# Two LayerNorms of the last four batches normalised on ScalarE, the routing maximum read from PSUM

## The chip, the cores and the metric

The kernel runs on one core of a Trainium2 chip. TensorE (PE) multiplies matrices, VectorE (DVE), ScalarE (ACT) and GpSimd (POOL) work element by element, and SyncE (SP) issues the DMAs. Each engine takes its instructions in the order in which the program gives them to it; between engines only semaphores order the work. The metric is the time of one execution on the device, in microseconds (us).

## The reference

Eight sequences (batches) of 128 tokens with 512 features pass through a two-layer decoder of six sublayers. Each sublayer is added to its input, and the sum is normalised over its features:

```python
def _layernorm(x, axis=-1, eps=1e-05):
    m = jnp.mean(x, axis=axis, keepdims=True)
    v = jnp.var(x, axis=axis, keepdims=True)
    return (x - m) / jnp.sqrt(v + eps)
...
    x = _layernorm(x + _L0_attn_ref(x, ...), axis=-1)              # stage 0
    x = _layernorm(x + _L0_xattn_ref(x, ctx_4096, ctx_4096), axis=-1)  # stage 1
    x = _layernorm(x + _L0_ffn_ref(x, ...), axis=-1)               # stage 2
    x = _layernorm(x + _L1_attn_ref(x, ...), axis=-1)              # stage 3
    x = _layernorm(x + _L1_xattn_ref(x, ctx_4096, ...), axis=-1)   # stage 4
    x = _layernorm(x + _L1_ffn_ref(x, L1_ffn_route_w, L1_ffn_A, L1_ffn_Bw), axis=-1)  # stage 5
```

Stages 4 and 5 matter here. Stage 4 is an attention with 32 query heads on 8 key and value heads, whose output is projected by `Wo`. Stage 5 sends each token to the one of eight low-rank experts with the largest logit:

```python
        logits = jnp.einsum('bsd,ed->bse', x, route_w)
        topk_v, topk_idx = jax.lax.top_k(logits, 1)
        route_weight = jax.nn.one_hot(topk_idx[..., 0], E, dtype=logits.dtype) * topk_v
        h = jnp.einsum('bsd,erd->bser', x, A)
        wh = route_weight[..., None] * h
        out = jnp.einsum('bser,eor->bso', wh, Bw) * SCALING
```

## The kernel before

The whole decoder is one program of five instruction streams, written out by hand; what stands in a stream is done in that order. `x_tok` holds all eight batches in SBUF, tokens on the 128 partitions and 512 features in the free dimension, and is updated in place by every stage. HB is 4, half of the batches.

Stage 4 runs in slots. Slot s, from 0 to 63, is one batch of one key head in one half of the batches (NU is 16 heads over both halves, so NU*HB is 64). The loop is pipelined over the slots on each engine: in slot s the scores of s are computed, the weights of s-1 are turned, the values of s-2 are multiplied and the projection by `Wo` of s-4 is added up in PSUM. The loop goes on to slot 71 (SLOTS is 72) to drain. In slots 64 to 67 the projections of the last four batches (4 to 7) are completed, and stage 5 of these batches runs in steps that `routed_at(s)` gives out, one batch after the other, a slot apart: step 0 turns x (PE line 883, ScalarE copies it out as `x5T`), step 1 multiplies by the experts' first matrices and the route (PE line 892), and DVE chooses the expert in `route` (lines 1971 to 1978), step 2 turns the weighted result `wh` (PE line 897, ScalarE copies it out as `whT`), step 3 multiplies by the second matrices (PE line 900), and DVE adds and normalises. Step 0 of batch 4 is in slot 65, step 3 of batch 4 in slot 68, that of batch 7 in slot 71. Within a slot the steps of the earlier batch come first. The first four batches go through the same steps one at a time in slots 40 to 55, beside the attention of the others.

A LayerNorm has two parts on DVE. `ln_a` adds the sublayer's result to x (line 1574), takes the statistics (1576, 1577) and adds epsilon to the variance (1578). POOL raises that to the power -0.5 in `rstd` (line 1322). `ln_b` waits for POOL and then subtracts the mean and multiplies (line 1582), in one instruction. In slots 64 to 71 `ln_b` follows its `ln_a` at once, so that DVE waits there for POOL. What else stands in DVE's stream there: `o_rest`, the rest of the attention's output that ScalarE's rounding leaves (line 1964), for s-2, at the head of slots 64 and 65. PE's step 0 of batch 4 waits for the last `o_rest` too:

```python
                    elif rb == HB and step == 0:
                        pe.wait_ge(S.t_sb, NU * HB)
                        pe.wait_ge(S.o_sb, NU * HB)
```

ScalarE's copies out of PSUM all go through one helper, so that the profile has them all at line 968; they are told apart by their tiles. `o_split` is the rounded part of the attention's output, and `x5T` and `whT` are parts of `arena` (128x512 and 128x128). SP stores each batch when its `x_done` has come (line 490), in order.

Of the kernel before, what the change touches and what calls it, by code (L numbers as in the profile page):

```python
# [15 lines left out]
P = 128  # L16
B = 8
# [115 lines left out]
def decoder_kernel(nc, xT, xtok, ctxT, ctxtok, par, rows, four, win, wx, wdt, wout, qw, sc, ze,  # L133
                   loraA, loraBT, dwin, dw1, dw2, dwout, wq, wk, wv, wo, ra, bwT, out):
    scratch = nc.dram_tensor("bc_scratch", [2, NS, HT], F32, kind="Internal").ap()
    with ExitStack() as ctx:
# [33 lines left out]
        lnmv = sb("lnmv", [P, B, 2])  # L170
        lnve = sb("lnve", [P, B])
        lnrs = sb("lnrs", [P, B])
        halfneg = sb("halfneg", [P, 16])

        def pc(name):
# [203 lines left out]
        def by_dve(k, c):  # L379

            return c == 1 and k % 4 == 2

        def weighed(k, c):

# [581 lines left out]
        def _(act):  # L966
# [304 lines left out]
            def routed(b, step, bk):  # L1271
# [6 lines left out]
                else:  # L1278
# [2 lines left out]
                        act.wait_ge(S.rf_ps, b)  # L1281
                    av(whT, bank[bk][:, 0:P], ACT.Identity).then_inc(S.whT_done, 1)

            for j in range(GQ):
                query_out(0, j)
                split_q(j + 3)
                if j % 2:
                    keys_values(KV_LAST + 3 + j // 2)
            for s in range(SLOTS):
# [16 lines left out]
                if 2 <= s < NU * HB + 2:  # L1306
                    r = s - 2
                    rv, rb = r // HB, r % HB
                    act.wait_ge(S.av_ps, r + 1)
                    if r >= 3:  # L1310
                        act.wait_ge(S.op_ps, r - 2)

                    av(osp[:, 0, r % 3, :], bank[3][:, :], ACT.Identity,
                       bias=pc("bv")[:, rv % NKV:rv % NKV + 1]).then_inc(S.o_hi, 1)
                for rb, step, bk in routed_at(s):
                    if step in (0, 2):
                        routed(rb, step, bk)

        def rstd(pool, stage, b):

# [4 lines left out]
        def _(pool):  # L1325
# [164 lines left out]
            for b in range(B):  # L1490
                rstd(pool, 3, b)
                if b >= HB:
                    rest_q(b - HB + 3)

            for s in range(SLOTS):
                if s < 2 * NKV * HB:
                    rest_q(s + 7)
                    rest_of(wos[:, 1, s % 8, :], wo_sb[:, s % 3, :], wos[:, 0, s % 8, :], S.wo_hi, s + 1, S.wo_lo)
                for b in range(B):
                    if s == (0 if b < HB else (NKV - 1) * HB) + b % HB:  # L1500
                        bias(b, 2 * B + b, "bo")
                rv, b = (s - 4) // HB, (s - 4) % HB
                if rv % NKV == NKV - 1 and 4 <= s < 2 * NKV * HB + 4:
                    rstd(pool, 4, (rv // NKV) * HB + b)
                for rb, step, bk in routed_at(s):
                    if step == 3:
                        rstd(pool, 5, rb)

        @block.vector
        def _(dve):  # L1510
# [56 lines left out]
            def ln_a(stage, b, ps, ready, value):  # L1567
# [7 lines left out]
                dve.wait_ge(S.x_sum, lnc(stage, b))  # L1575
                link(v.bn_stats(lnst[:, b, :], x_tok[:, b, :]))
                link(v.bn_aggr(lnmv[:, b, :], lnst[:, b, :]))
                v.tensor_scalar(lnve[:, b:b + 1], lnmv[:, b, 1:2], 1e-5, None, ALU.add).then_inc(S.ln_ve, 1)  # L1578

            def ln_b(stage, b):  # L1580
# [387 lines left out]
            def route(b):  # L1968

                dve.wait_ge(S.r_ps, b + 1)  # L1970
                link(v.tensor_copy(logits, bank[2][:, P:P + 8]))
                link(v.max(rt8, logits))
                link(v.max_index(ri8[:, :], rt8, logits))
                link(v.tensor_copy(rif, ri8[:, :]))
                link(v.tensor_scalar(rwt, pc("iota8"), rif[:, 0:1], rt8[:, 0:1], ALU.is_equal, ALU.mult))
# [8 lines left out]
            for s in range(SLOTS):  # L1984
# [8 lines left out]
                if 4 <= s < NU * HB + 4:  # L1993
                    r = s - 4
                    rv, rb = r // HB, r % HB
                    if rv % NKV == NKV - 1:
                        b = (rv // NKV) * HB + rb
                        ln_a(4, b, bank[4 + rb][:, :], S.op_ps, r + 1)
                        ln_b(4, b)
                for rb, step, bk in routed_at(s):  # L2000
                    if step == 1:
                        route(rb)
                    elif step == 3:
                        ln_a(5, rb, bank[bk][:, :], S.rf_ps, rb + 1)
                        ln_b(5, rb)


# [69 lines left out]
```

## Time and profile before

| | us |
|---|---|
| Median of 3 runs | 1402.76 |
| Lowest, highest | 1397.98, 1403.25 |
| The profiled execution | 1402.18 |
| Its span, from the first instruction to the last event | 1400.4 |
| PE busy in the span | 1289.2 (92%) |
| DVE busy | 927.4 (66%) |
| ACT busy | 731.3 (52%) |
| POOL busy | 646.5 (46%) |

The shares are averages over stages with different limits. A row of the timeline gives the start of an instruction from the start of the span, its duration, the engine, the line, the tiles that it writes and reads with their shapes, and in brackets how long the engine was idle before it and whose work ended that. A row of the table of windows gives busy time and number of instructions of each engine in one stretch; PEclk is the clock granted to TensorE as a share of its full 2.4 GHz. A matmul with 32-bit operands is shown as two records.

### The profile page before, as it was taken

The numbers are of one execution on the slowest core, as the hardware profiler recorded it, in microseconds if no ns is written. First come the engines' busy times: TensorE is split into PE (matmuls) and PEld (weight loads), VectorE is DVE, ScalarE is ACT, GpSimd is POOL, SyncE is SP. The second block draws the span as 40 slices with busy tenths as digits, with TensorE's granted clock in tenths as the row PEclk, the third lists the DMA queues.
The fourth block names the chain that finished last, engine by engine and source line by source line (L and its number), as shares of the span: only waits on it lengthen the run. The fifth ranks groups of instructions, "written<-read, shape, count | busy, mean of one in ns | idle before, by whom it ended". The sixth has DMA issues, their size and how long they took to land.

```text
span 1400.4 us, 18312 instructions
## 1 busy us (share of the span) xinstructions
PE 1289.2 (92%) x6432; PEld 929.4 (66%) x6432; DVE 927.4 (66%) x1690; ACT 731.3 (52%) x1407; POOL 646.5 (46%) x471
## 2 busy tenths in 40 slices
PE   7996887888899899989999999999998999999996
PEld 6874766666667664443655555778787778778774
DVE  4775898999988877795545535654444465555566
ACT  5579999899988841211232232544444335444441
POOL 4128988898888812213711113623332433333221
PEclk9998999999999999998999999999999999999999
DMA  5002200030000050003010000322121122112110
GB/s 176 8 25 91 91 1 1 31 135 17 1 1 1 1 175 17 16 1 98 13 70 23 1 30 23 121 68 75 61 76 60 61 76 76 61 61 72 42 53 30
DMA packets 29641, 71.45 MB, mean 51 GB/s; under 512 B 3408, under 2 KB 3664, under 8 KB 27632
## 3 DMA queue, kind: packets, MB, share of 16 engines
q1 hardware_dynamic: 29552, 70.30, 15.2%
q8 instruction: 52, 0.85, 0.3%
q14 instruction: 37, 0.30, 0.1%
HBM read 68.12 MB, written 2.16 MB: 50 GB/s over the span
## 4 chain that ended last, share of the span: by engine, by line
PE 67%; DVE 13%; ACT 10%; issue 5%; POOL 3%; DMA 1%; SPq 1%; DVEq 0%; POOLq 0%; ACTq 0%
PE psum L499 9%; PE psum L501 9%; PE psum L500 9%; ACT arena L968 6%; DVE arena L1672 4%; PE psum L574 4%; PE psum L916 4%; PE psum L776 4%; PE psum L943 4%; PE psum L770 3%; ACT psum L968 3%; PE psum L599 3%; PE psum L588 2%; PE psum L669 2%; PE psum L935 2%
## 5 line engine op out<-in xcount | busy, mean ns | idle before, releaser
L1672 DVE TENSOR_TENSOR_SCAN arena<-psum,arena 128x512 f32<-128x512 f32 x256 | 298.7, 1208 | 49.4 <-ACT psum L968 49.3
L1402 POOL TENSOR_TENSOR arena<-arena 128x1024 f32<-128x1024 f32 x128 | 300.5, 2370 | 46.9 <-DVE arena L1672 46.6
L1338 POOL TENSOR_TENSOR w_split<-arena,w_split 128x512 fp32r<-128x512 f32 x128 | 168.0, 1332 | 315.5 <-ACT w_split L968 315.4
L574 PE MATMUL psum<-prm,arena 128*128 128x128 f32 x1024 | 167.2, 290 | 67.8 <-DVE arena L1672 44.0
L574 PEld LDWEIGHTS psum<-prm,arena 128*128 128x128 f32 x1024 | 115.4, 145 | 136.7 <-DVE arena L1672 68.4
L968 ACT ACTIVATE arena<-psum,ssmC 128x256 f32<-128x256 f32 x448 | 179.8, 495 | 45.3 <-PE psum L574 45.2
L968 ACT ACTIVATE arena<-arena 128x512 f32<-128x512 f32 (+2 forms) x86 | 64.1, 749 | 224.9 <-DVE arena L1947 224.0
L968 ACT ACTIVATE arena<-psum 128x512 f32<-128x512 f32 (+2 forms) x164 | 92.4, 575 | 168.4 <-PE psum L720 48.4
L968 ACT ACTIVATE psum<-arena,amat 128x508 f32<-128x508 f32 x256 | 170.9, 726 | 0.5 <-DVE arena L1672 0.5
L968 ACT ACTIVATE arena<-psum,prm 128x512 f32<-128x512 f32 (+1 forms) x130 | 90.5, 708 | 134.2 <-PE psum L501 71.3
L588 PE MATMUL psum<-prm,arena 128*128 128x128 f32 x1024 | 137.7, 278 | 0.1
L499 PE MATMUL psum<-w_split,o_split 128*128 128x512 f32 x256 | 125.2, 489 | 0.0
L588 PEld LDWEIGHTS psum<-prm,arena 128*128 128x128 f32 x1024 | 120.1, 143 | 0.4 <-ACT arena L968 0.3
L499 PE MATMUL psum<-x_split,w_split 128*128 128x512 f32 x256 | 107.5, 420 | 1.4 <-DVE x_split L1933 1.4
L1322 POOL TENSOR_TENSOR lnrs<-lnve,halfneg 128x1 f32<-128x1 f32 x48 | 28.6, 596 | 168.8 <-DVE lnve L1578 168.8
L1964 DVE SCALAR_TENSOR_TENSOR o_split<-psum,prm,o_split 128x512 fp32r<-128x512 f32 x64 | 48.0, 749 | 86.6 <-ACT o_split L968 86.6
L501 PE MATMUL psum<-x_split,w_split 128*128 128x512 f32 x256 | 101.0, 394 | 0.0
L500 PE MATMUL psum<-x_split,w_split 128*128 128x512 f32 x256 | 100.7, 393 | 0.0
L501 PE MATMUL psum<-w_split,o_split 128*128 128x512 f32 x256 | 100.1, 391 | 0.0
L500 PE MATMUL psum<-w_split,o_split 128*128 128x512 f32 x256 | 99.8, 390 | 0.0
L1944 DVE TENSOR_REDUCE amax<-psum 128x4 f32<-128x512 f32 x64 | 44.0, 688 | 59.3 <-PE psum L916 59.1
L968 ACT ACTIVATE w_split<-arena 128x512 fp32r<-128x512 f32 (+1 forms) x129 | 74.6, 623 | 0.0
(225 smaller groups left out, 2361.9 us busy)
## 6 DMA issues: line engine op xcount, KB each, us to landing
arena<-wq SPq DMA_DIRECT2D x64, 256.0 KB, 2.5
arena<-wo SPq DMA_DIRECT2D x64, 256.0 KB, 2.9
arena<-bc_scratch SPq DMA_DIRECT2D x8, 1024.0 KB, 4.5
arena<-win SPq DMA_DIRECT2D x16, 256.0 KB, 4.3
arena<-xT SPq DMA_DIRECT2D x8, 256.0 KB, 5.9
x_tok<-xtok SPq DMA_DIRECT2D x1, 2048.0 KB, 10.5
arena<-wout SPq DMA_DIRECT2D x8, 256.0 KB, 5.7
arena<-ctxtok SPq DMA_DIRECT2D x1, 2048.0 KB, 8.0
```

What stands on the lines that cost most here:

```text
L499: mm(o, l[0], r[0], start=start, stop=False)
L500: mm(o, l[0], r[1], start=False, stop=False)
L501: return mm(o, l[1], r[0], start=False, stop=stop)
L574: last = nc.tensor.transpose(hT[:, c, b % 2, e, :], hst[:, (2 * k + e) % 4, b * L:(b + 1) * L], ident)
L588: last = mm(bank[6 + e][:, b * L:(b + 1) * L], hTs[:, k % 2, b, e, :], ident, start=(n == 0 and b == 0), stop=(n == NS - 1 and b == HB - 1 ...
L776: last = mm(o, ctxT_sb[:, b // HB, k, (b % HB) * L:(b % HB + 1) * L], wv_sb[:, k, c * 512:(c + 1) * 512], start=(k == 0), stop=(k == KD - 1))
L916: last = mm(bank[1][:, j * P:(j + 1) * P], qT[:, v % 2, j, b * L:(b + 1) * L], KT[:, v % NKV, gb * L:(gb + 1) * L], start=True, stop=True)
L943: mm(bank[3][:, :], V[:, (rv // NKV) * HB + rb, (rv % NKV) * P:(rv % NKV + 1) * P], pT[:, r % 2, :], start=True, stop=True).then_inc(S.av_ ...
L968: return nc.scalar.activation(o, i, f, **k)
L1338: gp.tensor_tensor(out_, whole, hi.bitcast(F32), ALU.subtract).then_inc(done, 1)
L1402: gp.tensor_tensor(bu[:, i % 4, :, :], dtu[:, (2 * j + e) % 4, :].unsqueeze(1).to_broadcast([P, NG, HT]), Brep[:, q * NG:(q + 1) * NG, :], ...
L1672: v.tensor_tensor_scan(hst[:, i % 4, :], bank[decay_slot(i)][:, :], bu[:, (k // NG * 2 + e) % 4, k % NG, :], 0.0, ALU.mult, ALU.add).then_ ...
```

## The change

For batches 4 to 7 in stages 4 and 5, `ln_b` leaves DVE. DVE computes the negated mean beside the variance (`lnneg`). POOL raises to the power -0.5 and then, in a second instruction that waits for the first, multiplies by the negated mean (`lnoff`). ScalarE computes x * scale + offset in place, with both as per-partition operands. The first four batches, and the stages 0 to 3, are left as they are. In `route`, for all eight batches, the maximum is taken from PSUM ahead of the copy of the logits, and no longer waits for it.

```diff
+        lnneg = sb("lnneg", [P, B])
+        lnoff = sb("lnoff", [P, B])
...
+        def by_act(stage, b):
+
+            return stage >= 4 and b >= HB
...
+            def normalise(stage, b):
+                act.wait_ge(S.ln_rs, lnc(stage, b))
+                av(x_tok[:, b, :], x_tok[:, b, :], ACT.Identity, scale=lnrs[:, b:b + 1],
+                   bias=lnoff[:, b:b + 1]).then_inc(S.x_done, 1)
...
                     av(osp[:, 0, r % 3, :], bank[3][:, :], ACT.Identity,
                        bias=pc("bv")[:, rv % NKV:rv % NKV + 1]).then_inc(S.o_hi, 1)
+                if NU * HB <= s < NU * HB + HB:
+                    normalise(4, s - NU * HB + HB)
                 for rb, step, bk in routed_at(s):
                     if step in (0, 2):
                         routed(rb, step, bk)
+                    if step == 3 and by_act(5, rb):
+                        normalise(5, rb)
...
+            def scale_offset(stage, b):
+                if not by_act(stage, b):
+                    return rstd(pool, stage, b)
+                pool.wait_ge(S.ln_ve, lnc(stage, b))
+                link(gp.tensor_tensor(lnrs[:, b:b + 1], lnve[:, b:b + 1], halfneg[:, 0:1], ALU.pow))
+                gp.tensor_tensor(lnoff[:, b:b + 1], lnneg[:, b:b + 1], lnrs[:, b:b + 1], ALU.mult).then_inc(S.ln_rs, 1)
...
                 link(v.bn_aggr(lnmv[:, b, :], lnst[:, b, :]))
+                if by_act(stage, b):
+                    v.tensor_scalar(lnneg[:, b:b + 1], lnmv[:, b, 0:1], -1.0, None, ALU.mult)
                 v.tensor_scalar(lnve[:, b:b + 1], lnmv[:, b, 1:2], 1e-5, None, ALU.add).then_inc(S.ln_ve, 1)
...
                 dve.wait_ge(S.r_ps, b + 1)
+                v.max(rt8, bank[2][:, P:P + 8])
                 link(v.tensor_copy(logits, bank[2][:, P:P + 8]))
-                link(v.max(rt8, logits))
...
-                        ln_b(4, b)
+                        if not by_act(4, b):
+                            ln_b(4, b)
...
-                        ln_b(5, rb)
+                        if not by_act(5, rb):
+                            ln_b(5, rb)
```

ScalarE's stream in slots 64 to 67 before: the turned weights of the last attention slot, the two last `o_split`, `x5T` of batches 4 and 5, `whT` of batch 4.

```order
L968 ACTIVATE arena<-psum 128x512
L968 ACTIVATE o_split<-psum,prm 128x512 x2
L968 ACTIVATE arena<-psum 128x512 x2
L968 ACTIVATE arena<-psum 128x128
L968 ACTIVATE arena<-psum 128x512
```

And the same place now:

```order
L974 ACTIVATE arena<-psum 128x512
L974 ACTIVATE o_split<-psum,prm 128x512
L974 ACTIVATE x_tok<-x_tok,lnoff,lnrs 128x512
L974 ACTIVATE o_split<-psum,prm 128x512
L974 ACTIVATE x_tok<-x_tok,lnoff,lnrs 128x512
L974 ACTIVATE arena<-psum 128x512
L974 ACTIVATE x_tok<-x_tok,lnoff,lnrs 128x512
L974 ACTIVATE arena<-psum 128x512
L974 ACTIVATE x_tok<-x_tok,lnoff,lnrs 128x512
L974 ACTIVATE arena<-psum 128x128
L974 ACTIVATE arena<-psum 128x512
```

The normalisation of batch 4 now stands between the two `o_split`, that of batch 5 ahead of `x5T` of batch 4, and that of batch 7 ahead of `whT` of batch 4.

ScalarE's stream in slots 68 to 71, which ends it, before: `whT` of batch 5, `x5T` of batch 7, `whT` of batches 6 and 7.

```order
L968 ACTIVATE arena<-psum 128x128
L968 ACTIVATE arena<-psum 128x512
L968 ACTIVATE arena<-psum 128x128 x2
L136 UNCONDITIONAL_BRANCH
```

And now:

```order
L974 ACTIVATE x_tok<-x_tok,lnoff,lnrs 128x512
L974 ACTIVATE arena<-psum 128x128
L974 ACTIVATE arena<-psum 128x512
L974 ACTIVATE x_tok<-x_tok,lnoff,lnrs 128x512
L974 ACTIVATE arena<-psum 128x128
L974 ACTIVATE x_tok<-x_tok,lnoff,lnrs 128x512
L974 ACTIVATE arena<-psum 128x128
L974 ACTIVATE x_tok<-x_tok,lnoff,lnrs 128x512
```

Each `whT` now stands behind the stage 5 normalisation of the batch before it.

DVE's stream in slot 68, with the LayerNorm of batch 4 in stage 5 and the choice of expert for batch 6, before:

```order
L1574 TENSOR_TENSOR x_tok<-x_tok,psum 128x512
L1576 BN_STATS lnst<-x_tok 128x6
L1577 BN_AGGR lnmv<-lnst 128x2
L1578 TENSOR_SCALAR lnve<-lnmv 128x1
L1582 TENSOR_SCALAR x_tok<-x_tok,lnmv,lnrs 128x512
L1971 COPY arena<-psum 128x8
L1972 MAX arena<-arena 128x8
L1973 MAX_INDEX ri<-arena 128x8
```

And now:

```order
L1596 TENSOR_TENSOR x_tok<-x_tok,psum 128x512
L1598 BN_STATS lnst<-x_tok 128x6
L1599 BN_AGGR lnmv<-lnst 128x2
L1601 TENSOR_SCALAR lnneg<-lnmv 128x1
L1602 TENSOR_SCALAR lnve<-lnmv 128x1
L1995 MAX arena<-psum 128x8
L1996 COPY arena<-psum 128x8
L1997 MAX_INDEX ri<-arena 128x8
```

The normalisation and its wait for POOL are gone from DVE, the negated mean is new, and the maximum and the copy have changed places.

## Rows read from the trace of the kernel before

**Rows 1.** Table of windows, three stretches: length, busy time by engine, PEclk, DMA.

```profile
1330.00:1362.00 32.00, 32.00 (x162) 25.00 (x160) 21.57 (x33) 14.04 (x25) 7.64 (x6) 1.00 0.17 58
...
1374.60:1383.30 8.70, 6.64 (x39) 4.97 (x37) 6.82 (x25) 1.47 (x3) 1.10 (x2) 1.00 0.00 0
1383.30:1397.95 14.65, 6.14 (x29) 3.47 (x29) 11.22 (x35) 1.43 (x4) 2.20 (x4) 0.86 0.14 54
```

**Rows 2.** Timeline of slots 64 to 66: start, duration, engine, line, tiles.

```profile
1367.38 0.69 DVE L1574 TENSOR_TENSOR x_tok<-x_tok,psum 128x512 f32<-128x512 f32 x1 [1.29 <-PE psum L501]
...
1368.23 0.69 ACT L968 ACTIVATE o_split<-psum,prm 128x512 fp32r<-128x512 f32 x1 [2.94 <-PE psum L943]
...
1369.28 0.55 POOL L1322 TENSOR_TENSOR lnrs<-lnve,halfneg 128x1 f32<-128x1 f32 x1 [7.16 <-DVE lnve L1578]
...
1370.33 0.75 DVE L1964 SCALAR_TENSOR_TENSOR o_split<-psum,prm,o_split 128x512 fp32r<-128x512 f32 x1
...
1371.17 0.63 PE L883 MATMUL psum<-prm,x_tok 128*128 128x128 f32 x4 [0.21 <-issue]
...
1371.56 0.48 PE L499 MATMUL psum<-w_split,o_split 128*128 128x512 f32 x1
...
1371.84 0.60 ACT L968 ACTIVATE arena<-psum 128x512 f32<-128x512 f32 x1 [2.91 <-PE psum L883]
...
1374.40 1.09 PE L892 MATMUL psum<-arena 128*128 128x136 f32 x8
```

**Rows 3.** Timeline of slots 67 to 71, the same columns.

```profile
1378.95 0.68 DVE L1574 TENSOR_TENSOR x_tok<-x_tok,psum 128x512 f32<-128x512 f32 x1
...
1383.30 0.68 DVE L1574 TENSOR_TENSOR x_tok<-x_tok,psum 128x512 f32<-128x512 f32 x1
...
1384.95 0.15 DVE L1578 TENSOR_SCALAR lnve<-lnmv 128x1 f32<-128x1 f32 x1
...
1385.19 0.55 POOL L1322 TENSOR_TENSOR lnrs<-lnve,halfneg 128x1 f32<-128x1 f32 x1 [3.80 <-DVE lnve L1578]
1385.77 0.55 DVE L1582 TENSOR_SCALAR x_tok<-x_tok,lnmv,lnrs 128x512 f32<-128x512 f32 x1 [0.66 <-POOL lnrs L1322]
...
1387.64 0.68 DVE L1574 TENSOR_TENSOR x_tok<-x_tok,psum 128x512 f32<-128x512 f32 x1
1387.78 0.33 PE L897 MATMUL psum<-prm,arena 128*128 128x128 f32 x1 [1.78 <-DVE arena L1978]
...
1392.49 0.28 ACT L968 ACTIVATE arena<-psum 128x128 f32<-128x128 f32 x1 [4.07 <-PE psum L897]
...
1392.82 1.12 PE L900 MATMUL psum<-arena 128*128 128x512 f32 x2 [0.37 <-ACT arena L968]
...
1394.92 0.68 DVE L1574 TENSOR_TENSOR x_tok<-x_tok,psum 128x512 f32<-128x512 f32 x1
...
1397.40 0.55 DVE L1582 TENSOR_SCALAR x_tok<-x_tok,lnmv,lnrs 128x512 f32<-128x512 f32 x1 [0.66 <-POOL lnrs L1322]
```

**Rows 4.** Timeline elsewhere: instructions like those that the change adds.

```profile
24.57 0.78 ACT L968 ACTIVATE arena<-psum,prm 128x512 f32<-128x512 f32 x1 [0.74 <-PE psum L501]
25.25 0.62 ACT L968 ACTIVATE arena<-arena 128x512 f32<-128x512 f32 x1
...
614.73 0.21 POOL L1438 TENSOR_TENSOR arena<-arena 128x4 f32<-128x4 f32 x1
615.02 0.21 POOL L1439 TENSOR_TENSOR arena<-arena 128x4 f32<-128x4 f32 x1
...
779.78 0.17 DVE L1866 TENSOR_SCALAR dve_<-dmv 128x4 f32<-128x4 f32 x1
779.86 0.42 DVE L1868 TENSOR_TENSOR arena<-arena,dmv 128x256 f32<-128x256 f32 x1
```

**Rows 5.** Timeline, matmuls in stretches where the granted clock was 0.50 or fell.

```profile
639.68 1.91 PE L662 MATMUL psum<-arena 128*128 128x512 f32 x2
...
1082.53 1.54 PE L849 MATMUL psum<-prm,x_tok 128*128 128x128 f32 x8 [2.60 <-DVE x_split L1933]
```

More of the change, by code:

```diff
@@ L1503, in _ @@
                 if rv % NKV == NKV - 1 and 4 <= s < 2 * NKV * HB + 4:
-                    rstd(pool, 4, (rv // NKV) * HB + b)
+                    scale_offset(4, (rv // NKV) * HB + b)
                 for rb, step, bk in routed_at(s):
                     if step == 3:
-                        rstd(pool, 5, rb)
+                        scale_offset(5, rb)
         @block.vector
```

## The prediction

> **What bounds the kernel now.** The change acts in the last 33 us (slots 64 to 71), and in `route` of the first four batches. I read first the table of windows. In the attention loop PE is busy for the whole 32 us [rows 1], so what DVE saves in `route` of the first four batches, under 0.2 us each, is hidden by PE: nothing. In the drain it is DVE that is busy (6.82 of 8.70 us, then 11.22 of 14.65), PE less than half in the second stretch, ACT and POOL hardly [rows 1]. Then the timeline, row by row. From 1378.95 on, the additions that open the LayerNorms follow each other at 1378.95, 1383.30 and 1387.64 [rows 3]: 4.35 us a slot, and between them DVE is never idle but for 0.66 us, in which POOL takes the root [rows 3]. So a slot is 2.47 us of `ln_a` and waiting (1383.30 to 1385.77), 0.46 of `ln_b`, 1.41 of `route`, all on DVE. Of the two last, 2.93 us apart, only one has no `route` behind it. Ahead of that PE sets the pace with the projections: the twelve matmuls of one are issued in 2.84 us (1371.56 to 1374.40) [rows 2], the last ends some 0.15 later, and what delays them delays all.
>
> The reader should see two loops: one that is there now (DVE alone), and one that the change builds (round four engines).
>
> **Part 1, what is removed and added on each engine.** DVE loses `ln_b` and its wait, 0.58 (1385.19 to 1385.77) and 0.46 us in each of eight LayerNorms. It gains the negated mean; a small instruction that waits for nothing starts the next 0.08 us later (779.78 to 779.86) [rows 4], so 0.07. In `route` one wait goes, under 0.15 us. POOL gains a small product that waits for the root: in the table of cosines such a one starts 0.08 us after the end of the one that it waits for (614.94 to 615.02) and takes 0.21 [rows 4]. So scale and offset are ready 0.55 + 0.08 + 0.21 = 0.84 us after POOL starts, not 0.55. From below the price is 0.15 (the least that small DVE instructions take, such as 1384.95 [rows 3]); from above it is another 0.55, the root's own price with the same shape [rows 3]. I take 0.21, the row with the same engine and operation. ACT gains eight `normalise`. No row shows one from SBUF with two per-partition operands. From PSUM a plain copy takes 0.60 [rows 2], one with both operands 0.78 [rows 4]; from SBUF a plain one takes 0.62 [rows 4]. I take 0.62 + 0.18 = 0.80 or 0.81, between 0.62 and 0.96 (the operands at twice the price). Back to back, the next starts 0.10 before the end (0.78 long, next after 0.68 [rows 4]). For a LayerNorm alone that is a loss: from the addition to `x_done` it was 2.47 + 0.55 = 3.02 us; now it is 1.89 from the addition to POOL (1383.30 to 1385.19 [rows 3]) + 0.07 + 0.84 + 0.05 to reach ACT (POOL to DVE took 0.03, 1385.74 to 1385.77) = 2.85 to the start of `normalise`, + 0.81 = 3.66.
>
> **Part 2, the new wait, and what is queued behind it.** ACT waits for POOL in its own stream, and four places stand behind that wait.
>
> (a) Slot 64. The last `o_split` starts at 1368.23 now, and is hidden [rows 2]. Behind `normalise` of batch 4 it starts at 1367.38 + 2.85 + 0.71 = 1370.94. DVE's `o_rest` follows at 1371.67 in place of 1370.33, and PE's turn of batch 4, which waits for that one, at 1372.47 in place of 1371.17 [rows 2]: 1.30 us late. PE does the projection of batch 6 only behind it, so that starts 1.30 late too.
>
> (b) Slot 65. `x5T` of batch 4 is now behind `normalise` of batch 5. The addition of batch 5 starts behind `o_rest`, at 1371.67 + 0.66 = 1372.33; + 2.85 = 1375.18; + 0.71 + 0.60 = 1376.49. PE would be ready for the first experts' product at 1374.40 [rows 2] + 1.30 = 1375.70 and waits until 1376.54: 2.14 late in all. The turn of batch 5 and the projection of batch 7 follow without a gap, 2.15 late. That projection ended at about 1374.40 + 1.24 (1.09 and 0.63, less 0.24 of overlap each, as 1371.17 to 1371.56 shows [rows 2]) + 2.84 + 0.2 = 1378.68, and DVE came to it at 1378.95 [rows 3]. Now the addition of batch 7 starts at 1380.87: 1.92 late.
>
> (c) Slot 67. `whT` of batch 4 waited for nothing but PE's turn, and was hidden. Now it stands behind `normalise` of batch 7: 1380.87 + 2.85 + 0.71 = 1384.43. The second product starts 0.33 later (1392.49 to 1392.82 [rows 3]), at 1384.76, and DVE adds 1.14 later, at 1385.90, in place of 1383.30: 2.60 late.
>
> (d) Slots 68 to 71. `whT` of each batch stands behind `normalise` of the batch before it, which waits for that batch's second product. This closes a loop: addition, statistics, root, product, `normalise` 2.85; + 0.71 to `whT`; + 0.33 to PE's second product; + 1.14 to the next addition = 5.03 us a batch. Three of them are 15.09; now the three intervals are 4.34 + 4.35 + 2.93 = 11.62 (1383.30 to 1394.92 [rows 3]). So 3.47 are lost. `route` and the first products fit beside this loop.
>
> (e) The last LayerNorm is 3.66 in place of 3.03 us (1394.92 to 1397.95 [rows 3]): 0.63 lost. The store behind it, 2.45 us to the end of the span, stays.
>
> The sum: 2.60 + 3.47 + 0.63 = +6.70 us.
>
> **Part 3, the clock.** PEclk is 0.86 over the last stretch [rows 1]: if full at first and then 0.50, it fell after 14.65 x (1 - 0.14/0.50) = 10.5 us, at about 1393.9, just behind PE's last product. PE was idle before it for 2.22 and 0.37 us. An idle stretch of 2.60 us is ahead of a matmul group in which the clock fell too [rows 5]. In the new loop PE has 1.5 to 2.8 us of work in 5.03, and is idle some 2.5 us before the second product of batch 5, 2.8 before batch 6's and nearly 4 before batch 7's. So I expect half clock for the last two of these. A product of that form took 1.91 us at clock 0.50 [rows 5] and 1.12 at full [rows 3], or 1.02 where nothing stood ahead of it: 0.8 to 0.9 each, on the path. Two are +1.7 to +1.8. The bounds are none of them and three, 0 and 2.7.
>
> The Trainium skill says much the same in words that would change the sign of the whole: Perfetto Trace Analysis, Optimizing Scalar/DVE Operations, states that if DVE is saturated, offloading work to Scalar may make sense. The trace bears out its condition, with DVE at 11.22 of 14.65 us, but not that what is offloaded lands beside the path; it is the second rival below.
>
> **The forecast**: 1402.18 + 6.70 + 1.8 = 1410.7 us, made against the profiled execution, which is 0.58 under the median of 1402.76. A measurement of this kernel can tell about 0.5% from no change, here 7.0 us, so the bound lies at 1409.8, and the forecast 0.9 above it.
>
> **Rivals.**
> First, the loop as above, but TensorE keeps its full clock, or loses it only before the last product: 1402.18 + 6.70 + 0 to 0.9 = 1408.9 to 1409.8. For it speaks that an idle stretch of 1.78 us before 1387.78 [rows 3] left the clock alone; against it, that the new ones are longer.
> Second, on the other side: faster. If an ACT that waits for POOL holds nothing that PE needs, that is if `whT` and `x5T` come in ACT's stream ahead of the `normalise` or their input comes later than it ends, then DVE alone is the loop, with 1.65 (1383.30 to 1384.95) + 0.08 + 0.07 of `ln_a` and 1.3 of `route`: 3.1 in place of 4.35 us. That saves 1.25 us in each of the four slots from 1378.95 on (5.0), and gives back 0.63 at the end and some 0.4 of waiting for PE: about -4.0, 1398.2. It decides where `wh` turned comes later than `normalise` of the batch before ends. For batch 6 it came at 1387.78 + 0.33 = 1388.11, where the LayerNorm of batch 5 ended at 1387.64 + 3.02 = 1390.66 [rows 3], so it is early, not late, and ACT's new order speaks against this rival.
> Third, the same loop with dearer parts: at a POOL product of 0.55 (+0.34) and `normalise` of 0.96 (+0.15), taken some seven times on the path ((a), (b) or (c), three of (d), (e)), +2.4 and +1.1 at most: up to 1414.2. At the low ends, 0.15 and 0.62: -0.4 and -1.3.
> Fourth, the change does nothing to the time: what DVE gives up, ACT takes, and the loops stay 4.35: 1402 to 1403. It would need the wait to be absent, as above.
>
> **How the numbers follow.** The forecast, with two products at half clock and prices near mine, gets 0.42; the first rival 0.27; the third, on its high side, 0.16; the second 0.06; the fourth 0.09 (with unseen shifts between executions, whose spread is 5.3 us before the change). Above 1409.8 lie three quarters of the first (0.32), a quarter of the first rival (0.07) and all of the third (0.16), so slower 0.55. Faster by over 7.0 us is in none of them but by chance: 0.02; the second rival is 0.3% and counts as the same. The rest is 0.43. The range goes from 1406.0 (low ends of both prices and no loss of clock: 1402.18 + 6.70 - 1.7 = 1407.2, and some of the spread) to 1414.0.
>
> **What would show it right or wrong.** In the changed trace: `normalise` with 0.80 us in 0.7 to 0.9; POOL's product 0.2 long; the last `o_split` more than 2 us later than 1368.2; PE idle and released by ACT before its second products; additions of stage 5 about 5.0 us apart, each behind a PE that ended just before; DVE idle more than ACT and POOL can explain by their work; PEclk 0.5 before the last product. I am wrong if the additions are 4.4 us or less apart, if DVE is still what releases PE's turn of `wh` on the chain that ended last, or if the part ahead of slot 64 has moved.

## The result and the profile after

The changed kernel takes 1407.95 us (median of 15 runs, 1403.77 to 1411.65), the kernel before, beside it, 1399.08 (15 runs, 1395.41 to 1403.25). The ratio is 1.0065 with a 95% interval of 1.0051 to 1.0079: 7 to 11 us slower. The profiled execution took 1409.42 us with a span of 1407.6; that of before 1402.18 with 1400.4.

Since single executions of one kernel differ by more than the change is worth, all that follows is measured in the **drain**: from the addition of batch 4 in stage 4 (the start of slot 64's LayerNorm) to the end of the last normalisation. Ahead of it both kernels do the same but for `route`, and what follows it, the last store, takes 2.4 to 2.5 us in all profiles. Before, the drain was 1367.38 to 1397.95, 30.57 us [rows 2, 3].

First the timeline of the changed kernel, as in [rows 2], slots 64 to 66 (start, duration, engine, line, tiles, and in brackets idle time and who ended it):

```profile
1366.58 0.69 DVE L1596 TENSOR_TENSOR x_tok<-x_tok,psum 128x512 f32<-128x512 f32 x1 [1.30 <-PE psum L507]
...
1368.55 0.55 POOL L1514 TENSOR_TENSOR lnrs<-lnve,halfneg 128x1 f32<-128x1 f32 x1 [7.23 <-DVE lnve L1602]
1369.17 0.19 POOL L1515 TENSOR_TENSOR lnoff<-lnneg,lnrs 128x1 f32<-128x1 f32 x1
1369.40 0.81 ACT L974 ACTIVATE x_tok<-x_tok,lnoff,lnrs 128x512 f32<-128x512 f32 x1 [4.90 <-POOL lnoff L1515]
1370.12 0.67 ACT L974 ACTIVATE o_split<-psum,prm 128x512 fp32r<-128x512 f32 x1
1370.82 0.75 DVE L1988 SCALAR_TENSOR_TENSOR o_split<-psum,prm,o_split 128x512 fp32r<-128x512 f32 x1 [2.35 <-ACT o_split L974]
...
1371.67 0.63 PE L889 MATMUL psum<-prm,x_tok 128*128 128x128 f32 x4 [1.50 <-DVE o_split L1988]
...
1374.29 0.81 ACT L974 ACTIVATE x_tok<-x_tok,lnoff,lnrs 128x512 f32<-128x512 f32 x1 [3.51 <-POOL lnoff L1515]
1375.01 0.57 ACT L974 ACTIVATE arena<-psum 128x512 f32<-128x512 f32 x1
...
1375.69 1.17 PE L898 MATMUL psum<-arena 128*128 128x136 f32 x8 [0.65 <-issue]
```

Here every link of wait (a) can be read: POOL's product, ScalarE's normalisation, and close behind it the `o_split`, DVE's `o_rest`, PE's turn. In place of 0.21 [rows 2] PE is now idle for 1.50 us before the turn. ScalarE itself was idle for 4.90 us before the normalisation, with the input of the `o_split` ready for about the last two of them (PE's last product with the values begins at 1366.38 and takes 1.02).

Then the same timeline in slots 68 to 71, which answers to [rows 3]:

```profile
1385.12 0.69 DVE L1596 TENSOR_TENSOR x_tok<-x_tok,psum 128x512 f32<-128x512 f32 x1 [1.88 <-PE psum L906]
...
1387.08 0.58 POOL L1514 TENSOR_TENSOR lnrs<-lnve,halfneg 128x1 f32<-128x1 f32 x1 [4.19 <-DVE lnve L1602]
...
1387.96 0.81 ACT L974 ACTIVATE x_tok<-x_tok,lnoff,lnrs 128x512 f32<-128x512 f32 x1 [3.58 <-POOL lnoff L1515]
...
1388.99 1.56 PE L906 MATMUL psum<-arena 128*128 128x512 f32 x2 [2.44 <-ACT arena L974]
...
1394.44 1.12 PE L906 MATMUL psum<-arena 128*128 128x512 f32 x2 [1.86 <-ACT arena L974]
...
1399.45 2.08 PE L906 MATMUL psum<-arena 128*128 128x512 f32 x2 [3.77 <-ACT arena L974]
1401.56 0.69 DVE L1596 TENSOR_TENSOR x_tok<-x_tok,psum 128x512 f32<-128x512 f32 x1 [4.07 <-PE psum L906]
...
1404.37 0.81 ACT L974 ACTIVATE x_tok<-x_tok,lnoff,lnrs 128x512 f32<-128x512 f32 x1 [4.98 <-POOL lnoff L1515]
```

DVE, which had no idle time here but the 0.66 us of POOL's root [rows 3], now stands still for up to 4.07 us until PE's second product; PE stands still until ScalarE's `whT`; ScalarE until POOL; POOL until DVE. Four engines wait for one another in a ring. The table of waits over the changed kernel's drain (engine and line, what it waits for: us in total, times, longest) says it in four rows:

```profile
POOL lnrs L1514 <- DVE lnve L1602: 36.4, 8, 7.2
ACT x_tok L974 <- POOL lnoff L1515: 31.0, 8, 5.0
...
PE psum L906 <- ACT arena L974: 10.5, 4, 3.8
DVE x_tok L1596 <- PE psum L906: 9.9, 4, 4.1
```

The windows of the changed kernel (length, busy time of PE, its weight loads, DVE, ACT and POOL, PEclk, DMA), in the two halves of the drain, beside [rows 1]: in the second half no engine is busy for even half of the 20 us.

```profile
1366.58:1385.12 18.54, 13.95 (x71) 10.54 (x70) 10.08 (x36) 5.45 (x9) 2.99 (x8) 1.00 0.00 0
1385.12:1405.18 20.06, 8.34 (x29) 4.54 (x27) 9.48 (x34) 4.22 (x8) 3.00 (x8) 0.70 0.10 39
```

The drain is now 1366.58 to 1405.18: 38.60 us, 8.03 longer. In us from its start:

| | before | forecast | changed | changed, again |
|---|---|---|---|---|
| addition of batch 5, stage 4 | 3.62 | 4.95 | 4.91 | 4.90 |
| addition of batch 7, stage 4 | 11.57 | 13.49 | 13.50 | 13.51 |
| additions, stage 5, batch 4 | 15.92 | 18.52 | 18.54 | 18.55 |
| batch 5 | 20.26 | 23.55 | 24.01 | 23.98 |
| batch 6 | 24.61 | 28.58 | 29.03 | 29.00 |
| batch 7 | 27.54 | 33.61 | 34.98 | 34.95 |
| end | 30.57 | 37.27 | 38.60 | 38.57 |

The forecast column is the prediction's sum without its clock term. What is left (0.46 at batch 5, none added at batch 6, 0.92 more at batch 7) is the clock's: the second products of batches 5 and 7 took 1.56 and 2.08 us in place of 1.12.

### The profile page after: what moved, and what is told of

It reads as the page before. It is cut to its first block, busy times and chain, and to the rows that moved or that the text cites. A ratio compares the mean times of both kernels' runs of the same rounds, so it can differ in the third digit from the quotient of the medians.

```text
span 1407.6 us, 18328 instructions
## 1 busy us (share of the span) xinstructions
PE 1288.4 (92%) x6432; PEld 927.7 (66%) x6432; DVE 923.3 (66%) x1690; ACT 736.2 (52%) x1415; POOL 647.2 (46%) x479
## 4 chain that ended last, share of the span: by engine, by line
PE 67%; DVE 13%; ACT 10%; issue 6%; POOL 3%; DMA 1%; SPq 1%; DVEq 0%; POOLq 0%; ACTq 0%
PE psum L505 9%; PE psum L507 9%; PE psum L506 9%; ACT arena L974 6%; DVE arena L1696 5%; PE psum L580 4%; PE psum L922 4%; PE psum L782 4%; PE psum L949 4%; PE psum L776 3%; ACT psum L974 3%; PE psum L605 3%; PE psum L675 2%; PE psum L941 2%; POOL arena L1417 2%
## 5 line engine op out<-in xcount | busy, mean ns | idle before, releaser
L1337 POOL TENSOR_TENSOR lnrs<-lnve,halfneg 128x1 f32<-128x1 f32 x40 | 24.2, 604 | 138.1 <-DVE lnve L1602 138.1
```

## The experiments

All ran beside the kernel before, and each is read by its drain first; the ratio to the kernel before follows. Two were executed only once, stage 4 alone (1404.14 us beside a median of 1398.34) and the one without the first wait (1408.06 beside 1399.15), and are read by the drain alone.

**ScalarE's normalisations later in its stream.** This is the test of the reason: same instructions, same engines, other places in one stream.

```diff
-                if NU * HB <= s < NU * HB + HB:
-                    normalise(4, s - NU * HB + HB)
+                if NU * HB < s <= NU * HB + HB:
+                    normalise(4, s - NU * HB - 1 + HB)
                 for rb, step, bk in routed_at(s):
                     if step in (0, 2):
                         routed(rb, step, bk)
+                for rb, step, bk in routed_at(s):
                     if step == 3 and by_act(5, rb):
                         normalise(5, rb)
```

> The changed kernel with the same instructions, but ScalarE's eight normalisations stand later in its stream: stage 4's one slot later, behind the last o_split, and those of stage 5 behind whT and x5T of their slot. Measured by the drain, from the addition of batch 4 in stage 4 to the end of the last normalisation: 30.57 us before, 38.60 changed. Theory A (what is queued behind ScalarE's wait costs the time): the drain falls to 26.1 us, additions of stage 5 are 3.1 us apart and then 2.0, and the execution is 4.5 us (0.3%) faster than before. Theory B (the normalisation itself, 3.66 us in place of 3.03 from addition to x_done, is what costs, 8 times 0.63 and the clock): the order is of no account, the drain stays at 36 us or more and the execution is 5 to 9 us slower than before.

Measured: drain 26.26 us; the additions of stage 5 at 14.50, 17.57, 20.64 and 22.64 from its start, 3.07, 3.07 and 2.00 us apart. Ratio 0.9975, interval 0.9963 to 0.9987; 1395.57 us (12 runs) against 1398.34. Its timeline in slot 69:

```profile
1373.58 0.81 ACT L974 ACTIVATE x_tok<-x_tok,lnoff,lnrs 128x512 f32<-128x512 f32 x1 [0.77 <-POOL lnoff L1516]
1373.61 0.29 DVE L2003 TENSOR_TENSOR arena<-psum,arena 128x128 f32<-128x128 f32 x1
1373.81 0.68 DVE L1597 TENSOR_TENSOR x_tok<-x_tok,psum 128x512 f32<-128x512 f32 x1
1373.95 0.33 PE L903 MATMUL psum<-prm,arena 128*128 128x128 f32 x1 [0.92 <-DVE arena L2003]
...
1374.32 0.28 ACT L974 ACTIVATE arena<-psum 128x128 f32<-128x128 f32 x1
...
1375.49 1.02 PE L906 MATMUL psum<-arena 128*128 128x512 f32 x2
```

The addition (L1597) has no idle time before it any more, PE's second product has none either, and the normalisation runs beside DVE's choice of expert. It is as long as in the changed kernel, 0.81 us, and POOL's product 0.19. Theory B falls: the longer LayerNorm alone does not make the kernel slower. From 38.60 to 26.26 us by order alone; 1.4 of the 12.3 is the clock, which here is full from the first addition to the last second product. Of the 4.3 us below the kernel before, some 0.5 is the step in `route`, if it is worth as much here as alone (below), and the rest the normalisations.

**Only the stage 5 part of the order put right.** Within a slot `whT` and `x5T` go ahead of stage 5's normalisation; stage 4 is left as changed.

```diff
                 for rb, step, bk in routed_at(s):
                     if step in (0, 2):
                         routed(rb, step, bk)
+                for rb, step, bk in routed_at(s):
                     if step == 3 and by_act(5, rb):
                         normalise(5, rb)
```

> Of the order only the stage 5 part is put right: within a slot whT and x5T come ahead of the normalisation of stage 5; stage 4 is as in the changed kernel. Theory A: the loop of slots 68 to 71 opens, stage 5 additions are 3.1 us apart in place of 5.04, the late start stays (first stage 5 addition 18.4 to 18.7 us after the drain's start, as in the changed kernel), drain 30.2 us, the execution within 1 us of the kernel before. Theory B: drain 36 us or more, additions still 5 us apart.

Measured: drain 30.28 us; the first stage 5 addition at 18.52, as late as in the changed kernel, then 3.08, 3.07 and 1.99 us apart. Ratio 1.0000 (0.9986 to 1.0014). The second product of batch 5 starts without any wait, where it stood behind 2.44 us of idle time in the changed kernel:

```profile
1387.10 1.02 PE L906 MATMUL psum<-arena 128*128 128x512 f32 x2
```

The two halves of the damage come apart: the ring of slots 68 to 71 is opened by these lines alone, and the 2.60 us lost ahead of it stay. This kernel loses 2.60 us in the first half of the drain and wins 2.89 in the second; its time alone would say that nothing had changed.

**Each stage alone.**

```diff
         def by_act(stage, b):
 
-            return stage >= 4 and b >= HB
+            return stage == 5 and b >= HB
```

with ScalarE's stage 4 calls left out in this one, and `stage == 4` in the other.

> Only stage 5 of the last four batches is normalised on ScalarE, stage 4 stays with VectorE. Theory A: start of the drain as before (first stage 5 addition 15.7 us after its start), then additions 5.0 us apart, drain 34.2 us with full clock and up to 35.8 where the granted clock halves before the second products; 3.6 to 5.2 us slower than before. Theory B: four longer LayerNorms, of which only the last is on the path: drain 31.2 us, or shorter since VectorE is relieved.

> Only stage 4 of the last four batches is normalised on ScalarE, stage 5 stays with VectorE. Theory A: the first stage 5 addition comes 18.5 us after the drain's start in place of 15.9 (waits behind the normalisations of batch 4, 5 and 7), then additions 4.25 us apart, drain 32.8 to 33.0 us, 2.3 us slower than before. Theory B: stage 4's four longer LayerNorms cost 0.63 each on the path, 2.5 us, at the same place; here the two theories hardly differ in size, but by A ScalarE releases TensorE late at the turn of batch 4 and at the first product of batch 4.

Measured, stage 5 alone: first stage 5 addition at 15.64, then 5.97, 5.15 and 5.95 us apart, drain 36.33; ratio 1.0042 (1.0022 to 1.0063). The second products of its last three batches, by the timeline:

```profile
1384.77 2.08 PE L906 MATMUL psum<-arena 128*128 128x512 f32 x2 [2.02 <-ACT arena L974]
...
1390.73 1.26 PE L906 MATMUL psum<-arena 128*128 128x512 f32 x2 [2.13 <-ACT arena L974]
...
1395.87 2.08 PE L906 MATMUL psum<-arena 128*128 128x512 f32 x2 [3.66 <-ACT arena L974]
```

Less what these take above 1.12 each (0.96 + 0.14 + 0.96), the intervals are 5.0, 5.0 and 5.0 and the drain is 34.27, the 34.2 of the sum. The 36.33 is above the 35.8 that was expected with the clock, since this execution lost more to it (2.06 us) than the changed kernel's profile. Stage 4 alone: additions at 4.91, 8.49, 13.50 and 18.53, the same as in the whole change to 0.02 us, then 4.22, 4.21 and 2.94 apart, drain 32.93, inside what was expected. Its last `o_split` starts at 1370.51, pressed to the end of the normalisation, and its turn follows at 1372.06 with 1.50 us of idle time before it, just as in the changed kernel. The parts add up: 34.27 - 30.57 and 32.93 - 30.57 are 3.70 and 2.36, and the whole at full clock is 38.60 - 1.40 - 30.57 = 6.63. The parts sum up to 6.06. What is missing is the gain of `route`: it shows only where DVE sets the pace, with stage 5 alone ahead of slot 68 (15.64 for 15.92, 0.28), with stage 4 alone behind it (the last three intervals 11.37 for 11.62, 0.25), and in the whole change nowhere, since DVE waits in both halves. Without it the parts give 6.59 of 6.63.

**The first of the four waits alone taken away.** The changed kernel, with one normalisation (batch 4, stage 4) moved behind the last `o_split`.

```diff
-                if NU * HB <= s < NU * HB + HB:
+                if s == NU * HB + 1:
+                    normalise(4, HB)
+                if NU * HB < s < NU * HB + HB:
                     normalise(4, s - NU * HB + HB)
```

> The changed kernel, with one ScalarE normalisation moved: that of batch 4 in stage 4 behind the last o_split instead of ahead of it. This takes away the first of the four waits that the prediction names, and leaves the others. By the sum: the second addition comes 3.6 to 3.7 us after the drain's start in place of 4.91, TensorE's turn of batch 4 is 1.25 us earlier, the first stage 5 addition at 17.2 in place of 18.5, the loop stays at 5.0, drain 1.25 us shorter: 35.9 us at full clock, up to 37.4 with the clock falling as in the changed kernel. If the later waits absorb it (batch 5's normalisation ahead of x5T decides alone), the first stage 5 addition stays at 18.5.

Measured: the second addition at 3.63, PE's turn of batch 4 3.89 us after the drain's start in place of 5.09 (1369.87 - 1365.98), the fourth addition at 12.24, the first of stage 5 at 18.23, drain 37.84. The 18.23 looks like the second outcome, but the row on PE's second product of batch 4 says what it is:

```profile
1382.09 2.08 PE L906 MATMUL psum<-arena 128*128 128x512 f32 x2 [2.44 <-ACT arena L974]
```

It was caught by the half clock, which it was not in the changed kernel: 18.23 - 0.96 = 17.27, where the sum has 17.2. The last one took 2.08 too, the two between 1.12: 37.84 - 1.92 = 35.92 for 35.9. With the clock the drain is 0.4 above the 37.4 that was expected at most, since this execution lost 1.92 us to it and not 1.4. The first wait is worth 1.2 to 1.3 us and is not absorbed by the later ones. A reader who took the addition alone would have drawn the wrong conclusion from it.

**Idle matmuls to hold the clock.** The changed kernel, with PE given work while it waits.

```diff
+                    for i in range({HB: 2, HB + 1: 2, HB + 2: 3, HB + 3: 4}.get(b, 0)):
+                        mm(bank[bk][:, :], ident, bw_sb, start=True, stop=True)
                     pe.wait_ge(S.whT_done, b + 1)
                     mm(bank[bk][:, :], whT, bw_sb, start=True, stop=True).then_inc(S.rf_ps, 1)
```

> The changed kernel with 2, 2, 3 and 4 idle matmuls (128x512, into the bank that the second product then overwrites) ahead of the second products of batches 4 to 7, where TensorE waits for ScalarE. Their results are thrown away; the output is unchanged. If the halved clock is part of the price: PEclk stays 1.00 until the last second product, each of these takes 1.0 to 1.1 us (1.12, 1.56, 1.12, 2.08 in the changed kernel), the drain is 37.0 to 37.3 in place of 38.60 us. If the clock is not on the path, or the added matmuls delay the real ones: 38.6 or more.

Measured: drain 37.22 us, additions of stage 5 5.04, 5.03 and 5.01 apart, ratio 1.0033 (1.0017 to 1.0048). All four second products take 1.12 or 1.13 us; two of them:

```profile
1381.45 1.12 PE L908 MATMUL psum<-arena 128*128 128x512 f32 x2 [0.69 <-ACT arena L976]
...
1386.48 1.12 PE L908 MATMUL psum<-arena 128*128 128x512 f32 x2 [0.72 <-ACT arena L976]
```

So the clock was 1.38 us of the 8.03, and 37.22 is the forecast without it (37.27) to 0.05. The ratios show a larger difference to the changed kernel than that (1.0033 and 1.0061 in one comparison, 3.9 us), but the intervals allow for 1.4.

**The changed kernel again.**

> The changed kernel once more beside the others, for the share of the clock: the sum gives 37.1 us of drain with TensorE at full clock, and each second product at half clock adds up to 0.95; the first profile had 1.4 of that (38.60). Another execution should lie between 37.1 and 39.7, with the difference to 37.1 equal to what its second products take above 1.1 us each; all else (additions 5.0 us apart, ScalarE the releaser) the same.

Measured: drain 38.57, second products 1.12, 1.52, 1.12 and 2.07; 38.57 - 0.40 - 0.95 = 37.22. Ratio 1.0061 (1.0038 to 1.0083).

**The routing maximum alone.**

```diff
-                link(v.tensor_copy(logits, bank[2][:, P:P + 8]))
-                link(v.max(rt8, logits))
+                v.max(rt8, bank[2][:, P:P + 8])
+                link(v.tensor_copy(logits, bank[2][:, P:P + 8]))
```

> The kernel before with the routing maximum read from PSUM ahead of the copy, alone. Each route is 0.11 us shorter; four of them are in VectorE's loop, so the drain is 30.1 to 30.2 in place of 30.57 us; the four in the attention loop are hidden by TensorE. In the time of an execution nothing that can be measured. A rival: reading PSUM costs the maximum more than the wait saves, then the drain is 30.6 or more.

Measured: drain 30.07 us, 0.50 less; stage 5 additions 4.22, 4.21 and 2.94 apart for 4.34, 4.35 and 2.93 before. The maximum takes 0.17 from PSUM, as it did from SBUF. The ratio is 1.0002 (0.9987 to 1.0017): a gain in the drain that no timing of the whole can show.

**The last LayerNorm back on VectorE.** With all normalisations late in ScalarE's stream, that of batch 7 in stage 5, behind which nothing waits, is done by DVE.

```diff
-            return stage >= 4 and b >= HB
+            return b >= HB and (stage == 4 or stage == 5 and b < B - 1)
...
                 dve.wait_ge(S.ln_rs, lnc(stage, b))
+                if stage == 5 and b == B - 1:
+                    dve.wait_ge(S.x_done, lnc(5, b) - 1)
```

> ScalarE's normalisations late in its stream, as in the run with that order, and the very last one (stage 5, batch 7) left to VectorE, where a LayerNorm alone takes 3.03 us and not 3.66. Theory A: drain 25.5 us, 0.6 less than with all eight on ScalarE and 5.1 less than before; 5 us (0.35%) faster than before. If the extra POOL product and the longer ScalarE instruction were hidden, nothing is gained by this edit and the drain is 26.1.

Measured: drain 25.67, additions to 0.01 as with all eight on ScalarE, the end 0.59 earlier. Ratio 0.9970 (0.9955 to 0.9985). It is the shortest drain of all, 4.90 us below the kernel before, and this version beats both kernels. Between it and the one with all eight on ScalarE (0.9975) the timings can't decide; the drain does.

**VectorE's own order, nothing on ScalarE.** The kernel before, with `route` between `ln_a` and `ln_b` in slots 66 to 69, and the maximum from PSUM. In short:

```diff
                         ln_a(4, b, bank[4 + rb][:, :], S.op_ps, r + 1)
-                        ln_b(4, b)
+                        if s < NU * HB + 2:
+                            ln_b(4, b)
...
                     if step == 1:
                         route(rb)
+                if NU * HB + 2 <= s < NU * HB + 4:
+                    ln_b(4, s - NU * HB + HB)
+                for rb, step, bk in routed_at(s):
+                    if step == 3 and rb >= HB:
                         ln_b(5, rb)
```

> The kernel before with VectorE's own order changed and nothing on ScalarE: in slots 66 to 69 route stands between ln_a and ln_b, so that it fills the 0.66 us in which VectorE waits for POOL, and the maximum is read from PSUM. If the wait for POOL can be had back without moving work, a slot is 1.8 + 1.3 + 0.5 = 3.6 us in place of 4.35 and the drain is 27.8 us, 2.8 less than before, against 26.3 with all the normalisation late on ScalarE: the time 2.8 us (0.2%) below the kernel before. If what counts is the load of VectorE and not its wait, or stage 4's later x_done holds TensorE's turns: 30 us or more.

Measured: drain 27.69 us, additions of stage 5 3.46 apart and the last 2.95, ratio 0.9977 (0.9959 to 0.9994). The last second product took 1.34 us, so 0.22 of the drain is the clock's. The timeline shows POOL's root under DVE's own work, and the normalisation without a wait:

```profile
1383.87 0.58 POOL L1322 TENSOR_TENSOR lnrs<-lnve,halfneg 128x1 f32<-128x1 f32 x1 [2.88 <-DVE lnve L1578]
1383.97 0.09 DVE L1973 MATCH_VALUE_LOAD ri<-arena 128x8 f32 x1
...
1384.99 0.54 DVE L1582 TENSOR_SCALAR x_tok<-x_tok,lnmv,lnrs 128x512 f32<-128x512 f32 x1
```

Of the 4.90 us that the best version wins 2.88 are to be had without a second engine. With the 0.50 of `route` taken from both, turning three calls round gives 2.4 of 4.4, an estimate from the two runs: still more than half.

## Why the prediction was right, point by point

**What bounds it.** The prediction read two regimes out of the rows, PE up to the projection of batch 7 and DVE behind it. Both held: the 1.20 us by which PE's turn came earlier without the first wait were 1.28 at the end of the drain, and DVE relieved of the normalisation runs at 3.07 us a slot when nothing else is in its way (forecast 3.1).

**Prices.** ScalarE's normalisation was put at 0.80 or 0.81 from a neighbour in PSUM with both operands; it takes 0.81 (one 0.82). (By the prediction's own rule its upper bound, the operands at twice the price, is 0.98 and not 0.96; nothing hangs on it.) The Trainium skill's ScalarE: Activation LUTs, What ACT_TABLE_LOAD costs, states 186 ns and 0.833 ns an element for an instruction with immediates, and some 93 ns more for each per-partition operand; an estimate from these figures for 512 elements and two operands is 0.80 us. The trace agrees, with 0.81. POOL's product: forecast 0.21, measured 0.19; the gap ahead of it 0.07 for 0.08. The negated mean costs DVE 0.07 to 0.08. From the addition to the start of the normalisation: 2.82 (1366.58 to 1369.40) for 2.85.

**The waits.** (a) The last `o_split` starts 3.54 us after the drain's start, forecast 3.56; the turn 5.09, forecast 5.09. (b) The first experts' product at 9.11, forecast 9.16, and behind ScalarE's copy as foreseen (that ends at 1375.58, the product starts at 1375.69). (c) First addition of stage 5 at 18.54, forecast 18.52. (d) Intervals at full clock 5.04, 5.03 and 5.01 in the run with idle matmuls, forecast 5.03. (e) From the last addition to the end 3.62, forecast 3.66. In sum 6.65 (that run: 37.22 - 30.57) for 6.70. That it is the order and not the load or the length was argued in the prediction from the order rows; the run with the late order shows it. Of the single waits, (a) and (d) were each taken away alone and (e) was read with the last LayerNorm on VectorE; (b) and (c) were taken away only together with the others, so their share is read from the rows.

**The clock** is the term that was wrong in its parts. The prediction expected half clock for the second products of batches 6 and 7, +1.8. In the profile batch 5's is hit in part and batch 7's wholly, and batch 6's not at all: 0.44 + 0.96 = 1.40. The windows show when it fell and rose:

```profile
1389.00:1390.00 1.00, 1.00 (x2) 0.48 (x3) 0.00 (x0) 0.43 (x1) 0.00 (x0) 0.77 0.37 141
1390.00:1391.00 1.00, 1.00 (x4) 0.65 (x3) 0.41 (x1) 0.00 (x0) 0.00 (x0) 0.50 0.33 121
1391.00:1392.00 1.00, 1.00 (x6) 1.00 (x6) 0.96 (x2) 0.00 (x0) 0.00 (x0) 0.50 0.00 0
1392.00:1393.00 1.00, 0.58 (x3) 0.26 (x2) 0.75 (x8) 0.00 (x0) 0.45 (x1) 0.52 0.00 0
1393.00:1394.00 1.00, 0.00 (x0) 0.00 (x0) 0.88 (x4) 0.58 (x1) 0.30 (x2) 1.00 0.00 0
```

PEclk is the third figure from the right. The clock (1.2 GHz at 0.50, 2.4 at 1.00) fell at about 1389.5, 0.5 us into the product that followed an idle stretch of 2.44 us, and was back by 1393. Before it rose, PE had been busy without a gap from 1388.99 to 1392.58, with the product of batch 5, the turn of batch 6's `wh` and the first product of batch 7. The prediction left out that it can come back between two falls, and it put a product at half clock at 0.8 to 0.9 us more where it is 0.96. It fell again between 1396 and 1397, in PE's longest idle stretch, and the last product pays in full. Nor does the length of the idle stretch say which product is hit, as the prediction took it: 2.44 us stood ahead of batch 4's product too (1383.95), and it ran at full clock in this profile and at half in the run without the first wait. That run has 2.84 us ahead of batch 6's, with full clock:

```profile
1393.09 1.12 PE L906 MATMUL psum<-arena 128*128 128x512 f32 x2 [2.84 <-ACT arena L974]
```

Executions are hit at batches 5 (in part) and 7 in both profiles of the changed kernel, at 4 and 7 without the first wait, at 5, in part 6, and 7 with stage 5 alone; the loss was 1.40, 1.35, 1.92 and 2.06 us. So with the ring in place and no idle matmuls the clock took 1.35 to 2.06 us in each of the four executions profiled, but never from the same products as forecast, and that 1.8 came near was in part luck.

**The time.** The forecast was 1410.7, measured 1407.95; but the three executions shown of the kernel before had a median of 1402.76, and all fifteen have 1399.08. Taken by itself 1407.95 is below the 1409.8 that the prediction named as the bound of slower; it is slower by 0.65% because the kernel before is faster than the prediction knew. As a difference, +8.5 was forecast from the profiled execution, +8.0 was the drain's, and +9.1 (7 to 11) is the ratio's. The choice between slower and the same was a near one, as the chances said (0.55 to 0.43), since the bound of 0.5% lies inside the terms' own uncertainty: without the clock's 1.4 us the run with idle matmuls comes to 1.0033.

**The rivals.** The first, full clock, did not come in either profile of the changed kernel. The second, faster by 4.0 where ScalarE's wait holds nothing, comes to 30.57 - 4.0 = 26.6 us of drain; the order that it asks for, once made, gives 26.26. The Trainium skill (Perfetto Trace Analysis, Optimizing Scalar/DVE Operations) states of operations that either engine can do that "if DVE is saturated, offloading some work to Scalar (or even GPSIMD) may make sense". The run with the late order agrees with it, with a drain 4.3 us below that of the kernel before. The changed kernel shows that the place in the other engine's stream decides. The third rival's dear prices and the fourth, no change, are ruled out by the rows: 0.19 and 0.81 us for the two parts, and additions 5.0 us apart and not 4.35.

## What to carry to other kernels

An instruction that is moved to another engine brings its wait along, and everything behind it in that in-order stream now waits for a chain that it had nothing to do with. So read what stands behind the new place and who waits for it, and put the moved instruction behind whatever of its slot feeds another engine; here the change cost 6.6 us at full clock with the eight instructions in one place and gave 4.3 with them in another. Where an engine waits in the middle of its own work, try first to put its next independent work into the gap.

Measure a change in the tail of a kernel by the tail: from an event ahead of it to the end of the last instruction, less what matmuls at half clock add. That gave differences of 0.05 us here, where medians of a dozen executions leave 2 us open.

## What the runs showed of the hardware that was not expected

The executions of one kernel spread over some 8 us. In the profiles the start of the drain moves as much: from 1359.31 us in that with the late order to 1367.38 in that of before, though the instructions ahead of it are the same but for `route`. What goes along with it is how long TensorE's clock was granted at half, added up from PEclk in windows of 1 us, here for all twelve profiles:

| profile | us at half clock ahead of 1360 | of these from 625 to 700 | start of the drain |
|---|---|---|---|
| late order | 34.1 | 6.8 | 1359.31 |
| maximum alone | 44.4 | 6.8 | 1363.13 |
| idle matmuls | 44.3 | 6.8 | 1364.09 |
| late order, last on VectorE | 44.3 | 6.8 | 1364.82 |
| stage 5 alone | 54.6 | 13.6 | 1365.27 |
| without the first wait | 47.8 | 6.8 | 1365.98 |
| changed | 51.2 | 13.6 | 1366.58 |
| stage 4 alone | 54.6 | 13.6 | 1366.97 |
| changed, again | 54.6 | 13.7 | 1367.16 |
| `route` between | 51.2 | 13.7 | 1367.19 |
| only stage 5's order put right | 54.6 | 13.6 | 1367.30 |
| before | 58.0 | 13.7 | 1367.38 |

One stretch can be compared instruction by instruction, at the end of stage 1 and the start of what follows. In the windows of the kernel before:

```profile
632.22:654.43 22.21, 19.96 (x33) 7.48 (x32) 12.24 (x30) 2.72 (x7) 4.48 (x13) 0.69 0.19 62
```

and from the same instruction to the same instruction with the late order:

```profile
627.54:646.40 18.86, 16.61 (x33) 6.48 (x32) 11.96 (x30) 2.71 (x7) 4.47 (x13) 0.82 0.18 58
```

Every engine does the same number of instructions. PE is busy for 3.35 us less at a granted clock of 0.82 in place of 0.69, and the stretch is 3.35 us shorter. So the same instructions are granted full clock for longer in one execution than in another. All twelve profiles fall into two groups here: from POOL's root at 613.75 us (of the kernel before) to that at 656.60 it is 42.84 to 42.86 us in the seven with 13.6 or 13.7 in the third column, and 39.46 to 39.51 in the five with 6.8. From there to the drain they agree to 0.21 us. Ahead of that first root they already differ by up to 6.7 us, and there half clock and time do not go in step: the kernel before and the run without the first wait have 37.5 and 34.1 us at half clock ahead of 530 and reach that root at 613.75 and 615.74. What makes that part, and why the clock is granted for longer in one execution than in another, stays open.
